# Graph attention over 8192 nodes: the residual made behind the first stage by ScalarE and TensorE, and a quarter of the adjacency's columns folded onto another before they are searched

## What is computed

```python
h = relu(layernorm(x)); out = x + gnn(h, adj)
# gnn:
h = (x @ W.T).reshape(n, H, D)
s_src, s_dst = einsum(h, a_src), einsum(h, a_dst)
attn = s_src[:, None, :] + s_dst[None, :, :] + adj[:, :, None] * We[:, 0] + be
attn = leaky_relu(where(adj > 0, attn, -inf), 0.2)
attn = softmax(attn, axis=1)
return einsum('ijh,jhd->ihd', attn, h).reshape(n, H * D) + x @ Wr.T + br
```

## Time and profile before

| | |
|---|---|
| median of 3 runs | 2309.33 us (2308.79 to 2314.66) |
| profiled execution | 2312.84 us, of which its span is 2310.8 us |
| DVE busy | 2024.3 us, 88% |
| POOL busy | 1595.9 us, 69% |
| ACT busy | 1115.5 us, 48% |
| PE busy | 1002.1 us, 43% |
| mean granted TensorE clock | 0.69 of full speed |
| DMA | 473.62 MB, mean 205 GB/s |

### The profile page before, as it was taken

One profiled execution on the slowest core, in us unless ns is written; L12 is line 12 of the kernel. 1 busy time (PEld: TensorE's weight loads), 2 busy tenths in 40 slices (PEclk: granted clock), 3 DMA queues, 4 the chain that ended last, 5 costly groups with the idle time before them and its releaser, 6 DMA issues. The chain is left out here.

```text
span 2310.8 us, 22965 instructions
## 1 busy us (share of the span) xinstructions
PE 1002.1 (43%) x3773; PEld 789.3 (34%) x3774; DVE 2024.3 (88%) x5351; ACT 1115.5 (48%) x4803; POOL 1595.9 (69%) x2020
## 2 busy tenths in 40 slices
PE   4767304522453194236332643353253336363343
PEld 3555203322432173225321532242242225242232
DVE  5899797899699789999888999999999998887942
ACT  2333205633574384446543654545354446485553
POOL 5544476777776777677777777777677774777775
PEclk9998656766675667667765766666666667676676
DMA  6444876667466757877777777777778885667333
GB/s 148 161 148 138 290 229 160 200 213 236 131 212 213 223 159 235 251 236 228 219 218 222 225 254 229 249 250 247 247 256 242 257 249 174 203 197 217 88 76 65
DMA packets 164570, 473.62 MB, mean 205 GB/s; under 512 B 35888, under 2 KB 54360, under 8 KB 164216
## 3 DMA queue, kind: packets, MB, share of 16 engines
q1 hardware_dynamic: 86088, 278.11, 36.6%
q0 software_dynamic: 78336, 194.09, 30.6%
HBM read 435.24 MB, written 36.83 MB: 204 GB/s over the span
## 5 line engine op out<-in xcount | busy, mean ns | idle before, releaser
L626 POOL DMA_INDIRECT arena<-table,arena x1262 | 1270.7, 1007 | 479.2 <-issue 322.1
L1347 PE MATMUL banks<-arena,ident 128*128 128x264 f32 x1566 | 500.2, 492 | 1161.9 <-DVE arena L939 1161.9
L1215 ACT ACTIVATE arena<-arena 128x32 f32<-128x32 f32 x3832 | 819.3, 307 | 2.2
L1347 PEld LDWEIGHTS banks<-arena,ident 128*128 128x128 f32 x1566 | 385.0, 251 | 1273.7 <-issue 1050.9
L772 DVE FIND_INDEX8 work<-work,adj_sb 128x8 uint32<-128x502 f32 (+56 forms) x775 | 667.2, 865 | 0.0
L783 DVE MAX8 work<-adj_sb 128x8 f32<-128x502 f32 (+56 forms) x775 | 652.4, 856 | 0.0
L1209 ACT ACTIVATE arena<-pre 128x104 f32<-128x104 f32 (+22 forms) x81 | 23.3, 304 | 910.1 <-DVE pre L929 909.6
L1353 PE MATMUL banks<-arena,ident 128*128 128x264 f32 x958 | 254.4, 408 | 42.5 <-ACT arena L1215 42.5
L939 DVE TENSOR_TENSOR arena<-arena 128x1024 f32<-128x1024 f32 (+8 forms) x169 | 226.4, 1389 | 51.3 <-ACT arena L1209 51.2
L1353 PEld LDWEIGHTS banks<-arena,ident 128*128 128x128 f32 x958 | 181.7, 197 | 103.6 <-ACT arena L1215 76.2
L1192 ACT ACTIVATE pre<-arena,we_all 128x13 f32<-128x13 f32 (+26 forms) x536 | 165.3, 406 | 87.3 <-DMA arena<-lists 87.0
(11 more groups left out here) (130 smaller groups left out, 966.2 us busy)
## 6 DMA issues: line engine op xcount, KB each, us to landing
adj_sb<-in_adj_dram SPq DMA_DIRECT2D x505, 512.0 KB, 4.4
arena<-table,arena POOLq DMA_INDIRECT x1262, 3.8
table<-arena POOLq DMA_DIRECT2D x32, 264.0 KB, 2.7
arena<-in_x_dram SPq DMA_DIRECT2D x32, 256.0 KB, 2.9
resid<-arena POOLq DMA_DIRECT2D x32, 256.0 KB, 2.6
out_dram<-arena POOLq DMA_DIRECT2D x32, 256.0 KB, 2.8
adj_sb<-in_adj_dram SPq DMA_DIRECT2D x1, 1536.0 KB, 23.5
lists<-arena,rank POOLq DMA_INDIRECT x67, 3.9
```

The costliest lines, as they stand in the source:

```text
L626: pool.indirect_dma_start(gath[0:n, un.slot(k), :], None, table[:, :], bass.IndirectOffsetOnAxis(ap=rec[0:n, k, 0:1], axis=0)).then_inc(la ...
L1215: last = s.activation(g, g, ACT.Copy, scale=gath[:, un.slot(k), HD + h:HD + h + 1])
L1347: last = m.matmul(ps_sum[:, u % 2, :], ident[:, :], gath[:, un.slot(k), :], start=(k == 0), stop=False)
```

## The change

The residual leaves the first stage. DVE, PE and POOL no longer make or write it there; `nmean` and `rstd` are kept for all 32 units, and their product `shift`. Behind the first stage ACT and PE make it in 64 steps, one for 128 rows: x is loaded again by ACT's queue, ACT applies Relu, PE transposes, ACT copies, PE adds x, br and the product with Wr in one PSUM bank, ACT copies it out and writes it twice. `RES_AT` places 32 steps ahead of unit 0's exponentials, 16 behind unit 0's and 16 behind unit 1's; both engines do them in their program order. Its buffers take 10 of the ring's slots, so that the first four laps of the ring have 76 slots (`LAPS`). POOL's deal of the first lists no longer waits for the writes of the first stage; the first gather waits for the table's.

From row block 7 on, columns 6144 to 8191 are folded onto 4096 to 6143: PE adds the near ones times 1 and the far ones times 2^-64 into four PSUM banks, and DVE scans these four banks of 512 instead of 4096 columns. `TURNS` shifts the far banks against the near ones, a number for each block, so that in no row two entries meet. `unfold` tells from the size whether a value came from near or far and restores value and column. ACT counts the entries of both halves with two passes of Sign (`see_fold`) and `fold_flags` compares. SP loads the half to be folded first, and for these pieces waits for ACT's passes of the block two before.

`SEGS` and `FOUND` are new: scans rise from 775 to 856, of which 228 are of banks; finds are placed two a unit up to unit 11, then 36 over 39 units, with none behind unit 56. `count(groups[0])` and its `ranks` move ahead of the first stage's last unit.

```diff
-SEGS = {1: (35, 2.3), 2: (26, 2.0), 3: (19, 2.0), 4: (17, 1.9), 8: (14, 2.1), 14: (12, 1.8), 16: (9, 2.0), 24: (9, 2.1), 32: (7, 2.0),
-        48: (7, 1.6)}
-FOUND = ((0, 7), (11, 26), (45, 60), (60, 67))
+LAPS = (76, 76, 76, 76)
+RES_AT = (32, 16, 16)
+SEGS = {1: (35, 2.3), 2: (26, 2.0), 3: (19, 2.0), 4: (17, 1.9), 7: (10, 1.8), 8: (9, 1.8), 11: (8, 1.9), 13: (7, 1.8),
+        23: (8, 1.8), 26: (7, 2.0), 28: (6, 1.8), 33: (5, 1.7)}
+FOUND = ((0, 7), (11, 28), (50, 64), (56, 67))
...
@@ SP: loads of the adjacency
-                for n in range(PIECES):
+                for i, n in enumerate(so.pieces):
...
+                    if sources[c - 2].folded and n * PIECE >= FOLD_AT:
+                        sp.wait_ge(S["fold_seen"], sources[c - 2].fold + 1)
+                    else:
+                        sp.wait_ge(S["scanned"], segs_before[c - 2] + scans_of(sources[c - 2], n))
...
@@ POOL: first stage and first lists
                     pool.wait_ge(S["hd_copied"], u + 1)
                     pool.dma_start(by_unit(table[PAD:PAD + N, :], u), hd_sb[:, q, :, 0:ROW]).then_inc(S[f"hd_out{q}"], 16)
-                    pool.wait_ge(S["res_done"], u + 1)
-                    nc.gpsimd.tensor_tensor(rt_sb[:, q, :, :], rt_sb[:, q, :, :],
...
-                    pool.dma_start(by_unit(resid, u), rt_sb[:, q, :, :]).then_inc(S[f"res_out{q}"], 16)
-                    pool.dma_start(by_unit(out, u), rt_sb[:, q, :, :]).then_inc(S[f"res_out{q}"], 16)
-            for b in range(2):
-                for q, each in (("hd_out", 16), ("res_out", 32)):
-                    pool.wait_ge(S[f"{q}{b}"], each * (UNITS // 2))
-
-            pool.wait_ge(S["pad_out"], 16)
...
             deal(groups[0])
             load_dealt(groups[0])
+            for q in range(2):
+                pool.wait_ge(S[f"hd_out{q}"], 16 * (UNITS // 2))
+            pool.wait_ge(S["pad_out"], 16)
+            pool.wait_ge(S["s_done"], UNITS)
@@ DVE: first stage, scan, keys
-                for b in range(2):
-                    last = v.scalar_tensor_tensor(out=rt_sb[:, q % 2, b, :], in0=ps_res[:, q % 2, b, :],
-                                                  scalar=rstd[:, q, b:b + 1], in1=x_sb[:, q, b, :],
-                                                  op0=ALU.mult, op1=ALU.add)
...
+            def unfold(so):
+                f = so.fold
+                vf, jf = val8[:, 0:8 * BANKS], jpad[:, 0:8 * BANKS]
+                v.tensor_scalar(fold_tag[:, :], vf, FOLD_SPLIT, 1.0 / FOLD_SCALE, ALU.is_lt, ALU.mult
+                                ).then_inc(S["tagged"], 1)
+                v.tensor_scalar(fold_one[:, 0, :], vf, FOLD_SPLIT, 0.0, ALU.is_ge, ALU.add,
+                                accum_out=fold_found[:, 0, f:f + 1])
+                v.tensor_scalar(fold_one[:, 1, :], vf, 0.0, 0.0, ALU.is_gt, ALU.add,
+                                accum_out=fold_found[:, 1, f:f + 1])
...
+                for lo, hi, far in ((0, cut, FOLD + BANK * so.turn), (cut, 8 * BANKS, BANK * so.turn)):
+                    if hi > lo:
+                        last = v.scalar_tensor_tensor(out=jf[:, lo:hi], in0=fold_tag[:, lo:hi],
...
+                v.scalar_tensor_tensor(out=vf, in0=fold_tag[:, :], scalar=1.0, in1=vf, op0=ALU.max, op1=ALU.mult
+                                       ).then_inc(S["unfolded"], 1)
...
@@ ACT: behind the first stage
+            def load_again(r):
+                act.dma_start(xr_sb[:, r % 3, :], x[bass.ts(r, P), :]).then_inc(S[f"xr_in{r % 3}"], 16)
+
+            def residual_step(r):
+                if r < TILES:
+                    act.wait_ge(S[f"xr_in{r % 3}"], 16 * (r // 3 + 1))
+                    if r >= 2:
+                        act.wait_ge(S["hr_turned"], r - 1)
+                    s.activation(hr[:, r % 2, :], xr_sb[:, r % 3, :], ACT.Relu, bias=shift[:, r // 2, r % 2:r % 2 + 1],
+                                 scale=rstd[:, r // 2, r % 2:r % 2 + 1]).then_inc(S["hr_done"], 1)
+                if 1 <= r <= TILES:
+                    act.wait_ge(S["hr_turned"], r)
+                    if r >= 3:
+                        act.wait_ge(S["res_ps"], r - 2)
+                    s.activation(hrT[:, (r - 1) % 2, :], ps_turn, ACT.Copy).then_inc(S["hrT_done"], 1)
+                if r >= 2:
+                    act.wait_ge(S["res_ps"], r - 1)
+                    if r + 1 < TILES:
+                        load_again(r + 1)
+                    if r >= 4:
+                        act.wait_ge(S[f"res_out{r % 2}"], 32 * (r // 2 - 1))
+                    s.activation(rt_sb[:, r % 2, :], ps_res, ACT.Copy).then_inc(S["res_copied"], 1)
+                    act.wait_ge(S["res_copied"], r - 1)
+                    act.dma_start(out[bass.ts(r - 2, P), :], rt_sb[:, r % 2, :]).then_inc(S[f"res_out{r % 2}"], 16)
+                    act.dma_start(resid[bass.ts(r - 2, P), :], rt_sb[:, r % 2, :]).then_inc(S[f"res_out{r % 2}"], 16)
...
+            def see_fold(so):
+                act.wait_ge(S["folded"], BANKS * (so.fold + 1))
+                for side in range(2):
+                    cols = adj_sb[:, so.buf, FOLD_AT + FOLD * side:FOLD_AT + FOLD * (side + 1)]
+                    last = s.activation(cols, cols, ACT.Sign, bias=tiny[:, :],
+                                        accum_out=fold_counts[:, side, so.fold:so.fold + 1])
+                last.then_inc(S["fold_seen"], 1)
...
             prepare(units[0])
+            for r in range(RES_AT[0]):
+                residual_step(r)
+            seen = 0
             for un in units:
                 if un.u + 1 < len(units):
                     prepare(units[un.u + 1])
+                while seen < found[un.u]:
+                    if sources[seen].folded:
+                        see_fold(sources[seen])
+                    seen += 1
                 exps(un)
+                for r in range(sum(RES_AT[:un.u + 1]), sum(RES_AT[:un.u + 2])):
+                    residual_step(r)
...
@@ PE
-                    for c in range(2):
-                        rows = hnT[:, q, b, c * P:(c + 1) * P]
-                        last = m.matmul(ps_res[:, q, b, :], rows, w_all[:, c, 272:528], start=(c == 0), stop=(c == 1))
...
+            def residual_step(r):
+                if r < TILES:
+                    pe.wait_ge(S["hr_done"], r + 1)
+                    if r >= 1:
+                        pe.wait_ge(S["hrT_done"], r)
+                    for c in range(2):
+                        last = m.transpose(ps_turn[:, c * P:(c + 1) * P], hr[:, r % 2, c * P:(c + 1) * P], ident[:, :])
+                    last.then_inc(S["hr_turned"], 1)
+                if r >= 1:
+                    q = (r - 1) % 2
+                    pe.wait_ge(S["hrT_done"], r)
+                    if r >= 2:
+                        pe.wait_ge(S["res_copied"], r - 1)
+                    m.matmul(ps_res, ident[:, :], xr_sb[:, (r - 1) % 3, :], start=True, stop=False)
+                    m.matmul(ps_res, ones[0:1, :], br_row, start=False, stop=False)
+                    for c in range(2):
+                        last = m.matmul(ps_res, hrT[:, q, c * P:(c + 1) * P], wr_all[:, c, :], start=False, stop=(c == 1))
+                    last.then_inc(S["res_ps"], 1)
...
+            def fold(so):
+                before = sources[so.c - 1]
+                for q in range(BANKS):
+                    near, far = FOLD_AT + BANK * q, FOLD_AT + FOLD + BANK * ((q + so.turn) % BANKS)
...
+                    if before.folded:
+                        pe.wait_ge(S["scanned"], segs_before[before.c] + q + 1)
+                    m.matmul(ps_fold[:, q, :], ident[:, :], adj_sb[:, so.buf, near:near + BANK], start=True, stop=False)
+                    m.matmul(ps_fold[:, q, :], small_ident[:, :], adj_sb[:, so.buf, far:far + BANK], start=False, stop=True
+                             ).then_inc(S["folded"], 1)
...
             for un in units:
+                while folds < min(len(sources), found[un.u] + 1):
+                    if sources[folds].folded:
+                        fold(sources[folds])
+                    folds += 1
                 tile_sums(un)
+                for r in range(sum(RES_AT[:un.u + 1]), sum(RES_AT[:un.u + 2])):
+                    residual_step(r)
```

238 lines of the change are left out of this document (172 added, 66 removed).

## The result

The changed kernel takes **2495.91 us**, median of 4 runs (2493.29 to 2500.83), against 2311.02 of the kernel before on the same chip: a ratio of **1.0801**, 95% interval 1.0778 to 1.0824. That is 185 us slower. The forecast was 2333, 22 us slower, and its range ended at 2405. The profiled execution has a span of 2494.6 us.

A forecast was written before the change was run, and what follows sets the result against it. POOL was taken as the bound from the first gather on. The profiled 2312.8 us, + 48.5 for POOL late behind the residual steps, - 25.0 for late stores, gave 2336.3; the runs' median 3.5 lower: 2333 us, range 2275 to 2405.

The forecast's parts named there:

- POOL is the path: From the first gather to the end POOL sets the time, occupied 96% between 599.3 and 1922 us.
- rows 5: Profile rows with two POOL stores waiting 10.92 and 14.11 us for DVE's evacuation; a faster DVE could return 25.0 us.
- rows 4: Profile rows of POOL gathers waiting for an earlier gather's landing, 109.1 us in 184 waits; costed at nothing.
- The 42 stores of the sum: Stores at 1.92 us each, 81 us of the 1272 us that POOL is occupied between 599.3 and 1922 us.
- Nothing on POOL, at most 15: The fold's work on TensorE and ScalarE was to cost POOL nothing, at most 15 us.
- M: The eight matmuls of one residual step on TensorE: 2.1 us at full clock, 3.8 at half.
- p: Time of one residual step: 3.5 us, bounds 2.5 and 5.3.
- a rival of 0.13: Residual steps crawl through slow loads or TensorE at 1.2 GHz: p = 4.6 us, 2406 us in all, chance 0.13.
- 324.7 + 66p: Start in us of unit 2's exponentials on ScalarE, behind the residual steps: 555.7 us forecast.
- exps(2): Unit 2's exponentials on ScalarE, queued behind the residual steps; start forecast at 555.7 us against 489.65 before.
- bank loop: Limit on a residual step from its one PSUM bank: M + copy 0.4 + issue 0.37 + 0.15 = 3.0 us.
- L: Landing time of a residual step's 128 KB load of x: at least 2.5 us, 2.9 used.

The follow-up runs named there:

- fold alone: The kernel before with only the fold added (new segments and find placing, residual in the first stage, ring of 86 slots): 2336.77 us, ratio 1.0085.
- the folds unused: The kernel before with TensorE folding row blocks from 7 on, far loads waiting for that, but DVE scanning all columns as before: 2317.01 us, ratio 1.0001.
- the useless matmul: The changed kernel with one unused 128-column matmul put where TensorE waits for the copy in each residual step: 2441.6 us, measured one time.
- the residual alone: The changed kernel with the fold undone, all 8192 columns scanned; residual steps, early deal and ring of 76 kept: 2483.38 us, ratio 1.0733.

## Why the prediction failed

**POOL is the path.** Right where it decided. A useful DVE relief of 160 us was to be worth the 25.0 us of rows 5 only, and 16.7 (fold alone) to 18 (the change) came back there. What I left out is that occupied POOL isn't a fixed pace: rows 4 were allowed to move "either way", costed at nothing, and moved by 50 to 65 us. Two readings were loose. The 42 stores of the sum are 40 and six shorter writes of partial blocks, which moves it by 4 us. And the gather of 1.09 us in rows 3 stands inside the weighting like the one of 2.23 (377.69 to 387.93); just behind it, at 389.05, one takes 0.95.

**The fold on DVE.** Right in size. Its busy time fell by 2032.3 - 1853.2 = 179 us from the folds unused to the folds used. Scans from PSUM cost what their columns do: 512 columns in 685 ns for MAX8 and 690 for FIND_INDEX8, where the 502 columns of rows 10 take 667.

```profile
L833 DVE MAX8 work<-banks 128x8 f32<-128x512 f32 x228 | 147.8, 685 | 70.3 <-PE banks L1565 70.3
...
L824 DVE FIND_INDEX8 work<-work,banks 128x8 uint32<-128x512 f32 x228 | 157.3, 690 | 0.0
```

**The fold on TensorE and ScalarE.** "Nothing on POOL, at most 15" failed. TensorE's part was cheaper than said (912 instructions, 502 us, 8.8 a block with nearly the least of 8.2 to 15.3) and ScalarE's in the range (two passes at 1.99 us a block):

```profile
L1564 PE MATMUL banks<-adj_sb,ident 128*128 128x512 f32 x456 | 255.6, 644 | 88.8 <-DMA adj_sb<-in_adj_dram 73.0
...
L1354 ACT ACTIVATE adj_sb<-adj_sb,tiny 128x2048 f32<-128x2048 f32 x114 | 227.2, 1994 | 34.3 <-PE banks L1565 32.8
```

Both cost nothing. The kernel loses on the other side: in the fold alone POOL lost 17.5 us between units 5 and 13 and 16.6 between 13 and 43, in longer waits for landings. Part of this comes with DVE's relief, which I had entered as pure gain; the rest is open.

**The first stage.** Wrong in our favour: the last centring began at 203.86 instead of 218.5, the first gather at 228.2 instead of 246. So the first stage became 15 us shorter than the 29 pairs of L753 at 0.87 us each account for; which of the things taken out of it (DVE's, TensorE's or POOL's part) gave the rest isn't shown. Deal to first gather took 14.6 us (16.6 forecast).

**The residual step, where the forecast broke.** The step that failed is the sentence "M is 2 x 1.03 = 2.1 us at full clock" and what was built on it: p = 3.5 us. Both rows of TensorE's price stood in rows 8, 1.91 beside 1.03, and the prediction gave 4.8 for half clock and kept it for a rival of 0.13. By its own formula 4.8 gives 2419 us, outside the range it stated; the rival and the range took 4.6. Measured: M = 4.34 and p = 5.3 in the median; of the 61 steps inside the three blocks 14 took longer than 5.4, up to 9.3, eight of them before 330 us. The formula itself, 324.7 + 66p for exps(2), gives with p = 5.3 and the start 18 us earlier 324.7 - 18 + 349.8 = 656.5; the trace has 658.5. The queue behind the steps was right too: exps(0), exps(1), exps(2), DVE's weighting, the ring. With the clock raised by the useless matmul, M is 2.38 and the step 3.25, so it is the clock that the sum had wrong, and not the loop. Even the rival was too cheap at p = 4.6, since it took M = 3.8; the 0.92 that the bank loop adds was right (0.96). The load was forecast well in the median of all steps (2.3 us, against 2.5 to 2.9), but not before 330 us, where it took 4.5.

```profile
arena<-in_x_dram ACTq DMA_DIRECT2D x64, 128.0 KB, 2.3
```

The Trainium skill's 2.0 us + bytes/436 GB/s (DMA: Bandwidth & Descriptors, "Anatomy of one DMA") is a fit for DMAs that GpSimd issues; used as an estimate for this load, which ScalarE issues, it gives 2.3. The trace agrees in the median, but not before 330 us (4.5), nor in the other kernels with the residual but for the residual alone (2.7 to 5.3). The prediction's "by it p would be 2.9" doesn't follow either: its bank loop of 3.0 holds no L, so p is at least 3.0 and the time 2300, not below 2294.

**From exps(2) on.** exps(2) to exps(4) took 100.2 us (forecast 90, before 113.5). The 90 was DVE's busy time of 93.9 with the changes added, as if its waits would all vanish.

**The sum as it came out.** By the second gather of unit 5, of which the prediction speaks: 166.2 there (forecast 48.5), + 18.5 to unit 13, + 17.5 to unit 43, - 18.2 at the end (forecast - 25.0) = 184.0, measured 184.9. Of the 160 us between this and the forecast's 23.5, 118 lie before that gather: 66 x (5.3 - 3.5) = 119 for the steps, 18 back for the start, 10 for exps(4), 2 that the formula misses, and 5 since the gather stands 8.3 us behind exps(4) and not 3.5. 36 are POOL's slower pace, and 7 the part of the 25.0 that didn't return. So the step makes three quarters of the miss, and the pace that was costed at nothing most of the rest. That the formula comes within 2 us is in part luck: late loads lengthened the first block by 13 us, while each block's first steps, which copy nothing yet or wait for nothing, are shorter than p.

## What to carry to other kernels

Work that moves off a first stage into one engine's program order is paid where it stands: the same 64 steps cost 192 us in three blocks ahead of the exponentials, and 18 to 24 in portions cut to that engine's free stretches (and in two banks). When a moved loop runs TensorE in short groups with a wait in each, cost it at TensorE's lower level first, and take the upper one only if nothing in the loop makes it wait. A helper engine made faster isn't a gain by itself where the bound engine waits for landings: look at what else changes with it (what is loaded, and when) before you count the few stores it may return.

## What the runs showed of the hardware

TensorE stayed at its lower level (1.2 GHz, granted clock 0.50) for 76 and 81 us on end while busy 90% of the time, with a wait of 0.53 us and some shorter ones in each step; one useless 128 x 128 matmul a step brought the first of these stretches to a granted clock of 0.84. DVE's MAX8 took 685 ns for 512 columns of a PSUM bank and 667 for 502 columns in SBUF, the same per column. TensorE read each adjacency block from row block 7 on beside DVE's scans, 400 us of matmuls in all, with no effect on the time (2317.01 us, 2316.25 before). And the fold, which makes DVE 179 us less busy, made the whole kernel 0.85% slower.
